# Flamingo block: the output projection in four parts of two pairs, through the score bank

## The reference

```python
x = x + tanh(g_xattn[0]) * xattn(_layernorm(x), ctx_1024, ...)
x = x + tanh(g_ffn[0]) * ffn(_layernorm(x), gate_w, w1, w2)
# xattn
xn = _layernorm(x, ln_gamma, ln_beta)
q = (xn @ w_q).reshape(B, SQ, 16, 64)
k, v = jnp.split(context @ w_kv, 2, axis=-1)
attn = softmax(einsum('bqhd,bkhd->bhqk', q * SCALE, k))
out = einsum('bhqk,bkhd->bqhd', attn, v).reshape(B, SQ, 1024)
return (out @ w_out + b_out) * tanh(gate[0])
# ffn: each token goes to the expert of its largest logit (8 experts, 160 places each)
h = relu(expert_input @ w1); expert_output = h @ w2
out = probability of the expert * its output row
```

## Time and profile before

| | |
|---|---|
| median of 3 runs | 470.92 us |
| lowest, highest | 470.62, 475.55 us |
| the profiled execution's own time | 470.09 us |
| its span | 467.8 us |
| granted TensorE clock, mean | 0.995 |
| PE / ACT / DVE / POOL busy | 89% / 83% / 77% / 76% |

### The profile page before, as it was taken

One profiled execution on the slowest core, in us unless ns is written; L12 is line 12 of the kernel. 1 busy time (PEld: TensorE's weight loads), 2 busy tenths in 40 slices (PEclk: granted clock), 3 DMA queues, 4 the chain that ended last, 5 costly groups with the idle time before them and its releaser, 6 DMA issues.

```text
span 467.8 us, 13169 instructions
## 1 busy us (share of the span) xinstructions
PE 414.6 (89%) x5096; PEld 267.4 (57%) x5096; DVE 361.4 (77%) x790; ACT 387.3 (83%) x632; POOL 353.6 (76%) x270
## 2 busy tenths in 40 slices
PE   7877889997999989999999999998999999878993
PEld 5443555655655556655655556655565565548892
DVE  4788787887978887888887897888888888885622
ACT  5988978899888988899988998898899998892330
POOL 3785877888788878888878887898888877871325
PEclk9999999999999999999999999999999999999998
DMA  5499999999999999999999999999999998996021
GB/s 171 150 183 194 201 191 177 166 191 192 195 180 200 203 194 182 189 188 194 215 190 208 188 195 202 189 193 203 186 182 184 193 184 153 167 191 127 15 68 45
DMA packets 283037, 82.10 MB, mean 175 GB/s; under 512 B 264387, under 2 KB 280435, under 8 KB 282976
## 3 DMA queue, kind: packets, MB, share of 16 engines
q1 hardware_dynamic: 281600, 77.96, 94.9%
q0 software_dynamic: 1376, 3.30, 2.1%
HBM read 10.83 MB, written 5.14 MB: 34 GB/s over the span
## 4 chain that ended last, share of the span: by engine, by line
PE 29%; DVE 24%; ACT 21%; DMA 10%; issue 8%; POOL 6%; SPq 0%; POOLq 0%; ACTq 0%; DVEq 0%
DVE MXL L915 10%; DMA PT<-PARTS 9%; ACT P L763 8%; ACT PARTS L773 6%; POOL PARTS L653 5%; DVE HL L901 4%; DVE VL L908 3%; PE psAB L1248 3%; ACT HL L724 3%; PE psX L1333 3%; PE psX L1369 3%; PE psO L1281 3%; PE psO L1283 2%; PE psO L1282 2%; PE psEF L1507 2%
## 5 line engine op out<-in xcount | busy, mean ns | idle before, releaser
L653 POOL TENSOR_TENSOR PARTS<-P,PARTS 128x1024 f16<-128x1024 f32 x125 | 265.7, 2131 | 61.1 <-ACT PARTS L773 60.7
L773 ACT ACTIVATE PARTS<-P 128x1024 f16<-128x1024 f32 x126 | 136.0, 1080 | 0.6
L763 ACT ACTIVATE P<-psAB,NB 128x512 f32<-128x512 f32 x128 | 81.5, 694 | 36.0 <-DVE NB L918 35.4
L1281 PE MATMUL psO<-VH,PT 128*128 128x65 f16 x1008 | 99.1, 194 | 10.6 <-DMA PT<-PARTS 9.9
L915 DVE TENSOR_REDUCE MXL<-psAB 128x2 f32<-128x1024 f32 x64 | 78.3, 1223 | 31.0 <-PE psAB L1248 15.4
L1281 PEld LDWEIGHTS psO<-VH,PT 128*128 128x128 f16 x1008 | 92.2, 98 | 13.6 <-DMA PT<-PARTS 11.8
L1282 PE MATMUL psO<-VL,PT 128*128 128x64 f16 x1008 | 99.0, 192 | 0.0
L1283 PE MATMUL psO<-VH,PT 128*128 128x65 f16 x1008 | 98.9, 193 | 0.0
L1282 PEld LDWEIGHTS psO<-VL,PT 128*128 128x128 f16 x1008 | 91.4, 98 | 1.4
L1283 PEld LDWEIGHTS psO<-VH,PT 128*128 128x128 f16 x1008 | 91.5, 97 | 0.0
L763 ACT ACTIVATE P<-psCD,NB 128x512 f32<-128x512 f32 x128 | 81.6, 702 | 0.1
(11 more groups left out here) (216 smaller groups left out, 794.3 us busy)
## 6 DMA issues: line engine op xcount, KB each, us to landing
ctx_raw<-in_ctx_dram SPq DMA_DIRECT2D x8, 256.0 KB, 4.2
w1s<-in_L_ffn_w_dram SPq DMA_DIRECT2D x8, 256.0 KB, 3.3
w2s<-in_L_ffn_w_dram SPq DMA_DIRECT2D x8, 256.0 KB, 3.4
PT<-PARTS SPq DMA_TRANSPOSE x126, 5.3
experts_table<-zeros POOLq DMA_DIRECT2D x2, 645.0 KB
X<-in_x_dram SPq DMA_DIRECT2D x8, 128.0 KB, 4.2
wraw<-in_L_xattn_w_kv_dram SPq DMA_DIRECT2D x4, 256.0 KB, 5.2
out_dram<-row SPq DMA_DIRECT2D x8, 128.0 KB, 2.3
```

The costliest lines, as they stand in the source:

```text
L653: pool.tensor_tensor(PARTS[:, par, qt, 1], P32[:, par, qt], PARTS[:, par, qt, 0], ALU.subtract).then_inc(plo_done, 1)
L763: last = act.activation(P32[:, par, qt, SK * h:SK * h + SK], score_bank(qt)[:, SK * h:SK * h + SK], ACT.Exp, bias=NB[:, par, qt, h:h + 1])
L773: act.activation(PARTS[:, hp % 2, qt, 0], P32[:, hp % 2, qt], ACT.Copy).then_inc(phi_done[qt], 1)
L1281: pe.matmul(psO[:, g:g + DH + 1], phi, VH[:, kt, head, 0:DH + 1], start=first_, stop=False)
```

## The change

The projection of a batch is made in four parts of two pairs. Pairs 0 and 1 are projected in slot 5 and pairs 2 and 3 in slot 7 of the same batch, pairs 4 and 5 in slot 1 and pairs 6 and 7 in slot 3 of the next. A part stands behind `values` in PE's row and ahead of the value projection; it is written to the first score bank psAB, once the slot's exponentials have read it, and the scores of the next slot wait until DVE has added it. DVE adds behind `normalise_heads`. The context's transposes stand in slot 3 (PE: behind the output's transposes, ahead of the values), its high part on ACT behind the first `phi`, its low part on DVE behind the keys' low part; the value projection of slot 2 stands last there as in other slots, and SP's load of the next context stands at slot 4. POOL adds the bias in slot 2, behind its low parts. Besides what the title says, POOL makes the high part of P for qt = 0 of pair 4 of each batch (`POOL_PHI`), which ACT made before. In the last batch pairs 2 and 3 are projected behind the last slot, where pairs 0 to 3 were.

```diff
-        PART_STEP, CTX_STEP, PROJECT_STEP = 1, 2, 3
+        CTX_STEP, PROJECT_STEP = 3, 3
+        PROJECTIONS = {5: (0, 0, (0, 1)), 7: (0, 1, (2, 3)), 1: (1, 2, (4, 5)), 3: (1, 3, (6, 7))}
+        POOL_PHI = (4,)
+        def pool_phi(j, qt):
+            return qt == 0 and j % PAIRS in POOL_PHI and j < LAST
+        def added(b, part):
+            if part == N_PARTS - 1:
+                return x1_done, B - 1 + QT if is_last(b) else b + 1
+            return part_done, b * (N_PARTS - 1) + part + 1
-        BO_STEP, BIAS_STEP = 2, 7
+        BO_STEP, BIAS_STEP = 2, 2
...
 # POOL
+                        if pool_phi(j, qt):
+                            pool.tensor_copy(PARTS[:, par, qt, 0], P32[:, par, qt]).then_inc(pool_phi_done, 1)
+                            pool.wait_ge(pool_phi_done, j + 1 - act_phis(j, qt))
...
 # DVE, behind normalise_heads
+                    if projection(b, hp):
+                        of, part, _ = projection(b, hp)
+                        if part < N_PARTS - 1:
+                            add_part(of, part)
+                        else:
+                            add_attention(of)
...
 # PE, in scores and in batch
+                if j and qt == 0 and projection(*back(b, hp, 1)):
+                    pe.wait_ge(*added(*projection(*back(b, hp, 1))[0:2]))
...
-                    if hp == PART_STEP and not is_first(b):
-                        project_part(b - 1, range(PAIRS // 2))
-                    if hp == CTX_STEP:
-                        v_project(*v_group(b, hp))
-                    if hp == PROJECT_STEP and not is_first(b):
-                        project(b - 1)
+                    if hp == CTX_STEP and not is_last(b):
+                        ctx_transposes(b + 1)
...
+                    if projection(b, hp):
+                        pe.wait_ge(exp_done, 2 * j + 1)
+                        of, _, pairs = projection(b, hp)
+                        project_part(of, pairs)
```

More of the change, by code:

```diff
@@ L352, in whole, with act_phis @@
             return j >= PAIRS - 1 and j % PAIRS in WHOLE
+        POOL_PHI = (4,)
+        def pool_phi(j, qt):
+            return qt == 0 and j % PAIRS in POOL_PHI and j < LAST
+        def act_phis(j, qt):
+            return sum(not pool_phi(p, qt) for p in range(j + 1))
         def split_pairs(j):
@@ L362, in gated_block, with projection, part_of @@
         PIECES = {3: 2, 6: 1}
-        PART_STEP, CTX_STEP, PROJECT_STEP = 1, 2, 3
+        CTX_STEP, PROJECT_STEP = 3, 3
+        PROJECTIONS = {5: (0, 0, (0, 1)), 7: (0, 1, (2, 3)), 1: (1, 2, (4, 5)), 3: (1, 3, (6, 7))}
+        N_PARTS = len(PROJECTIONS)
+        def projection(b, hp):
+            behind, part, pairs = PROJECTIONS.get(hp, (0, 0, ()))
+            if not pairs or b < behind or (is_last(b) and hp == PAIRS - 1):
+                return None
+            return b - behind, part, pairs
+        def part_of(pair):
+            return pair * N_PARTS // PAIRS
+        def added(b, part):
+            if part == N_PARTS - 1:
+                return x1_done, B - 1 + QT if is_last(b) else b + 1
+            return part_done, b * (N_PARTS - 1) + part + 1
         VALUES_BEHIND = 2
@@ L803, in batch @@
                         tokt_copy(b - 1)
-                    if j < LAST:
+                    if j < LAST and not pool_phi(j, 0):
                         phi(b, hp, 0)
+                    if hp == CTX_STEP and not is_last(b):
+                        ctxt_hi(b + 1)
                     exps(b, hp, 1)
@@ L810, in batch @@
                         phi(b, hp, 1)
[L811 removed]
+                    if v_group(b, hp):
                         v_hi(*v_group(b, hp))
@@ L1323, in last_transposes, with project_part @@
                 last.then_inc(p_psum, 1)
-            def project_part(b, pairs, bank=psX):
-                if bank is psX:
-                    wait_x((part_done, b + 1))
+            def project_part(b, pairs, bank=psAB):
                 pe.wait_ge(ot_done, b * PAIRS + pairs[-1] + 1)
@@ L1360, in project_last @@
                                          stop=(pair == pairs[-1]))
[L1361 to L1371 removed]
+                last.then_inc(part_psum, 1)
             pe.wait_ge(ident_ready, 1)
@@ L1449, in batch @@
                     values(b, PAIRS - 3)
-                    project_part(b, range(PAIRS // 2))
+                    wait_x(added(b, 1))
+                    project_part(b, (2, 3), psX)
                     values(b, PAIRS - 1)
```

70 lines of the change are left out of this document (26 added, 44 removed).

## The result

The changed kernel took 479.0 us (median of 5 runs, 477.75 to 482.05) against 471.61 of the kernel before beside it: ratio 1.0165, 95% interval 1.0125 to 1.0205. By the ratio it is 7.8 us slower (the two medians lie 7.4 apart), and it is outside the forecast range of 461 to 477. The profiled execution took 482.05 us, with a span of 480.2; it is the slowest of the five, 12 us above the profiled execution of before, so what is read off this pair of traces is larger than the 7.8 us.

A forecast was written before the change was run, and what follows sets the result against it. Five resources were taken as within a few per cent, the wait ending last in each slot deciding. Batch 0 +0.4, batches 1 to 6 +1.0, last batch -2.0, end -1.0: -1.6 on 470.92 gives 469.3 us, range 461 to 477.

The forecast's parts named there:

- Clean slots: Batch 6, nearly free of transpose waits: its eight slots were forecast to sum to 50.25 us, against 50.24 before.
- The terms for slot 3: Slot 3: ScalarE's late start 2.9 us plus the chain through VectorE's add, 8.15 less 0.05 overlap: 8.1 us (+1.1).
- The cast: Slot 4, POOL casting one high part of 1024 elements: taken as 1.1 us, near a MEMSET, not 2.13.
- the price of the queue: Context load just ahead of pair 4's transposes: 0 to 1.2 us on pair 4, 0.3 taken; about +1 us over batches 1 to 6.
- its own signs of being wrong: Slot 3 under 7.5 us, the cast over 1.5 us, or the transpose wait under 5 or over 15 us.
- POOL's 0.3 for the bias: Bias moved from slot 7 to slot 2, leaving POOL no idle stretch until slot 5: 0.3 us put on pair 5.
- the forecast +1: Pair 5 landing 0.6 us later for slot 7: +0.1 to 0.2 per batch, about +1 us over batches 1 to 6.
- 0.85 us won: Slot 1, with half the projection gone from PE's row: 6.55 us, a change of -0.85.
- The slower rival: POOL and the DMA queue become the bound at pair 5, read in slot 7: 474 to 480 us, typically 476; chance 0.24.
- The relief of PE: ScalarE not late in slot 3 (7.4 us, not 8.1), half the transpose wait gone: 459 to 465, typically 463; chance 0.30.
- The ends: Batch 0 +0.4 us, last batch without a context -2.0, half a projection gone behind the last slot -1.0.

The follow-up runs named there:

- undoing all three moves: Changed kernel with the context load in slot 1, the next batch's bias in slot 7 and no cast on POOL: 475.56 us, ratio 1.0067.

## Why the prediction was wrong

**Clean slots, right.** Eight slots forecast within 0.1, from the rows of before alone; PE released by the add of DVE (0.16 us behind X L995 in slot 0's row), as worked out. (The terms for slot 3 add up to 8.16 and not 8.15, which changes nothing.)

**The cast, right in size.** 1.1 taken, 1.04 measured. The Trainium skill ("GPSIMD Engine Reference", 4.1 Engine selection) puts an operation with one input at about line rate and one with two inputs at about half the speed of VectorE; 1.04 us beside 2.13 us for the same 1024 elements agrees.

**The step that failed is the price of the queue.** The prediction put it so: "it costs pair 4 between 0 and 1.2 us; I take 0.3", and "+0.1 to 0.2 in each of batches 1 to 6, about +1 us". The load and the bias together cost 5.9 us in the changed kernel and 6.1 in the one before, and batches 1 to 6 of the profiled execution got 12.5. Of its own signs of being wrong, the wait for the transposes over 15 us came true (17.8). The sum took each delay by itself and followed one pair into one slot.

First, the size of the delay. The load was priced by its issue, 0.85 us for it and 1.13 for two others. The queue is busy as long as its bytes move: 256 KB at about 190 GB/s, what the page's slices show in full batches, is 1.4 us as an estimate, three loads in a row 4 us. The Trainium skill ("DMA: Bandwidth & Descriptors", Queues, rings and completion order) says that each DMA engine takes the descriptors of one issuing queue in their order; SP's rows above show transposes and loads in one such row, and that moving two loads away gives the 7 us back agrees with it. Pair 4's way grew by 0.7 us, inside the range of 0 to 1.2 and over twice the 0.3 that was taken; POOL's 0.3 for the bias was right in size. In the kernel before it grew by 0.2 with the load alone, which is near the 0.3, and by 1.0 with load and bias. The sum took the two as if neither changed what the other costs.

Second, and of more weight, the readers. Only pair 5 was followed, into slot 7, with 0.4 us of its delay hidden beside DVE's chain. There the profiled execution got 4.1 us over six batches, of which two falls are some 3, so that the wait itself came out near the forecast +1. But pair 4 is read in slot 6, which got 4.6, and pair 7 in slot 1, which got 4.7, with one fall in each. Pairs 4, 5 and 6 are all 0.7 later, since the transposes behind a late one find no gap before pair 7. Pair 7 isn't later: slot 1 reads it 2.6 us earlier after its start (the first values matmul at 2.60 instead of 5.21 us), because the half projection no longer stands ahead of the values. The prediction counted that as 0.85 us won and didn't ask whether pair 7 was there; in batches 5 and 6 it was not, and the waits of 2.16 and 2.17 us arose.

Third, the half clock, which the sum had no term for: some 6 of the 12.5 us of the profiled execution, 2 to 3 of the 7.8 us by the mean clocks, both as estimates.

**The slower rival.** Its name and range (474 to 480) were right, and its place, pair 5 read in slot 7, for a third of the lateness. Its condition was not: it was to decide against the change from a cast of 1.4 us on. The cast took 1.04, and alone it costs nothing that can be told; the rival came true by the load and the bias. That 479.0 lies in its range is in part luck, since the terms that made the range (a cast of 2.13 us, the load at 1.2) are not those that came. The condition was hung on the one unknown duration, and not on the order in the queue that the diff itself showed.

**The relief of PE.** No part of it came: slot 3 took 8.02 wherever nothing was late, and ScalarE took up its exponentials 2.8 us after the scores of that slot (batch 6, 353.34 to 356.11), 2.9 forecast.

**The ends.** Batch 0: +0.8, +0.4 taken. Last batch: -1.5, -2.0 taken. The part behind the last slot: -1.0 taken. It is 52.2 us before and 52.9 after with a fall in it (from 432.76), and 52.1 in the kernel with load and bias moved and no fall there. The half projection did leave PE's row, and next to nothing came of it. The chain of before has it at

```profile
423.44 1.87 PE psX L1333 x16
```

and the chain of the other kernel, 2.9 us later throughout, goes there by ScalarE and VectorE:

```profile
423.77 0.28 ACT OT L788
424.05 0.92 ACT wraw L855
424.99 1.44 DVE wraw L1055 x2
```

A parallel path of equal length was hidden behind the row that was made shorter.

**What stays open.** Whether the late completions beside packets of the instruction queue can be avoided, and what they cost; the clock's share beyond the estimate from the mean clocks; and why undoing all three moves leaves less gain than load and bias alone is only argued from slot 5.

## What to carry to other kernels

When a step is moved in a full DMA queue, price its DMA by its bytes at the rate the queue reaches, add what stands next to it in the same order, and follow the delay to every reader behind it until a gap comes. Do the same when a reader is moved earlier: ask whether what it reads is there. Equal work in another order cost 8 us here, and one line that moved two loads to where the queue has gaps gave back 7 and made the kernel before faster too. A longer wait in the profile is not a loss by itself (the cast: 7 us more wait, no time): look at the slot lengths.

## What the runs showed that was not expected

TensorE's clock fell to its 1.2 GHz level inside a kernel in which PE is busy 88%, inside or behind waits of 1.99, 2.51 and 2.17 us, once behind two of under 0.6, and did not fall behind one of 2.16, nor in other kernels behind 2.56 (changed, bias in slot 7) and 2.47 (changed, no cast on POOL). So the length of the last wait does not tell whether it falls. A fall cost about 1.5 us, as much as the wait that came before it. In the records of the runs the mean clock is 0.979 to 0.993 for the changed kernel and 0.985 to 0.998 for the one before.

The four longest waits of the changed kernel for the transposes ended with completions that came about 2 us after the last packet of the data instead of 0.6, each with a 16 KB packet of the instruction queue started about 2 us before; such a packet stood ahead of the longest waits of the kernel before too.
